# Merged attention heads transposed by TensorE in the query steps, and the first half of feed-forward begun two steps sooner

## The reference

```python
Q, K, V = heads(Wq) / 8, heads(Wk) / 8, heads(Wv)             # heads(W) = x @ W.T, split in 16 heads of 64
def features(z):                                              # 256 features of each token and head
    xw = einsum('bhtd,hmd->bhtm', z, proj)
    xw = xw - max(xw, axis=-1)
    return exp(xw) * exp(-0.5 * sum(z * z)) + 1e-6
phiQ, phiK = features(Q) / 16, features(K) / 16
KV, Ksum = einsum('bhtm,bhtd->bhmd', phiK, V), sum(phiK, axis=2)
num = einsum('bhtm,bhmd->bhtd', phiQ, KV)
den = einsum('bhtm,bhm->bht', phiQ, Ksum) + 1e-6
merged = (num / den) as [tokens, 1024]
x = layernorm(x + merged @ Wo.T + bo)
x = layernorm(x + relu(x @ W1 + b1) @ W2 + b2)
```

## Time and profile before

| | |
|---|---|
| median of 3 runs | 1596.62 us (1596.11 to 1597.07) |
| the profiled execution | 1597.37 us |
| its span, core 2, the slowest | 1595.8 us |
| spans of the eight cores | 1586.9 to 1595.8 us |
| PE busy | 96% of the span |
| ACT, DVE, POOL busy | 46%, 43%, 35% |
| start of step 32, 36, 41, 42, 45 on PE (core 2) | 352, 393.9, 450.1, 461.2, 549.8 us |
| last `up()` ends | 1145.9 us |

### The profile page before, as it was taken

The page is one execution under the profiler, slowest core; times in us unless marked ns, Lnnn a source line. Parts: engine busy times, 40 slices in busy tenths (PEclk is TensorE's granted clock), DMA queues, the critical chain, the costliest instruction groups (busy, mean ns, idle before and its releaser), DMA issues.

```text
span 1595.8 us, 27925 instructions; the slowest of 8 cores (1586.9 to 1595.8 us)
## 1 busy us (share of the span) xinstructions
PE 1535.7 (96%) x9631; PEld 723.0 (45%) x9816; DVE 679.3 (43%) x1385; ACT 729.6 (46%) x1663; POOL 556.5 (35%) x471
## 2 busy tenths in 40 slices
PE   7999999997988899999999999999999999999998
PEld 3455555553434344444444444444444444444443
DVE  4788888887864444444444443100011111111111
ACT  3577777776764555656655565344311111011111
POOL 4466666662435443444434433000021111111110
...
GB/s 183 135 122 108 105 107 130 72 37 135 203 208 208 205 135 195 121 192 139 146 179 132 152 152 186 80 142 152 130 244 161 150 59 165 165 102 123 60 53 40
DMA packets 259433, 219.94 MB, mean 138 GB/s; under 512 B 205280, under 2 KB 205792, under 8 KB 255840
## 3 DMA queue, kind: packets, MB, share of 16 engines
...
## 4 chain that ended last, share of the span: by engine, by line
PE 86%; DMA 4%; DVE 3%; issue 3%; SPq 2%; ACT 2%; POOL 0%; DVEq 0%; ACTq 0%; POOLq 0%
PE bk L73 50%; PE ps L73 35%; SPq L68 2%; DVE maxa L80 2%; DMA eta<-eq 1%; ACT eq L74 1%; DMA wk<-WkT 1%; DMA etb<-eq 1%; ACT e L74 1%; DVE bia L79 0%; DMA x0f<-xT 0%; DVE r L79 0%; DMA r<-x 0%; SPq L62 0%; DMA r1n_d<-r1n 0%
## 5 line engine op out<-in xcount | busy, mean ns | idle before, releaser
L80 DVE TENSOR_REDUCE maxa<-ps 128x4 f32<-128x1024 f32 x256 | 311.5, 1217 | 118.9 <-PE ps L73 118.4
L74 ACT ACTIVATE eq<-ps,bia 128x256 bf16<-128x256 f32 x512 | 200.6, 476 | 218.8 <-DVE bia L79 108.6
L74 ACT ACTIVATE e<-ps,bia 128x256 bf16<-128x256 f32 x512 | 202.4, 487 | 89.0 <-DVE bia L79 85.5
L73 PE MATMUL bk<-rt,w 128*128 128x512 bf16 x1022 | 241.4, 381 | 0.7 <-issue 0.2
L73 PE MATMUL ps<-rt,w 128*128 128x512 bf16 x981 | 234.7, 381 | 3.2 <-issue 1.3
L73 PE MATMUL ps<-w,ht 128*128 128x512 bf16 x1004 | 222.6, 379 | 1.1
L73 PE MATMUL bk<-w,ht 128*128 128x512 bf16 x1003 | 222.4, 379 | 1.1
L74 ACT ACTIVATE jnk<-out,nmu 128x1024 bf16<-128x1024 f32 x32 | 36.7, 1148 | 383.6 <-DVE nmu L78 383.6
L77 POOL TENSOR_TENSOR out<-rn,b2b 128x1024 f32<-128x1024 bf16 x32 | 68.2, 2136 | 361.3 <-DMA out<-out 334.1
L78 POOL TENSOR_SCALAR eq<-eq 128x1024 bf16<-128x1024 bf16 x88 | 92.1, 1046 | 238.3 <-ACT eq L74 238.1
L78 POOL TENSOR_SCALAR e<-e 128x1024 bf16<-128x1024 bf16 x128 | 133.9, 1046 | 104.6 <-ACT e L74 99.6
...
## 6 DMA issues: line engine op xcount, KB each, us to landing
h_d<-hts SPq DMA_DIRECT2D x112, 256.0 KB, 2.6
ht<-h_d SPq DMA_DIRECT2D x14, 2048.0 KB, 15.2
...
r1n_d<-r1n SPq DMA_DIRECT2D x32, 256.0 KB, 2.8
w<-W POOLq DMA_DIRECT2D x4, 2048.0 KB, 16.4
```

The source lines that it names most:

```text
L73: "matmul": lambda g, *a, **k: g.matmul(*a, **k),
L74: "activation": lambda g, *a, **k: g.activation(*a, **k),
L80: "reduce_max": lambda g, *a, **k: g.reduce_max(*a, **k),
```

## The change

Five things, all written into the same lists of instructions:

1. `S_UP` goes from 42 to 40. Steps 40 and on have `up()`: two in step 40, four in step 41, then eight. `up()` 1 to 30 are done by the end of step 44, where 16 were; 42 remain behind step 66, where 56 did. `load_w1`, `load_rt` and the other things tied to `S_UP` move two steps up (`rt0` is loaded at the end of step 39, where it was step 40).
2. `w_step(r)` is r+3 where it was r+4. For the five blocks whose `wo` then falls before step 40 (r = 32 to 36), `transpose_m` is replaced by `transpose_pe`: 8 PE transposes against an identity (`IDN`) into bank 5, and one ACT copy of 128x1024 to `MGT`, at the start of the step of `wo`.
3. In the steps 32 to 39 the projections stand in groups 0 and 1 (they were in 0 and 2) and `wo` in groups 2 and 3 (1 and 3).
4. `eps_row` is spread over the four groups of step 33, in banks 5 and 6 in turn.
5. `warm` has 58 matmuls for 40, and the four W2 loads are issued after 2, 14, 26 and 38 of the 42 last `up()` (8, 20, 32 and 44 of 56).

```diff
@@ -476,14 +479,18 @@
-    S_UP = 42
+    S_UP = 40
 
     def n_step(r):
         return r + 2 if r <= S_UP - 2 else r + 1
 
     def w_step(r):
-        return {S_UP - 3: S_UP, S_UP - 2: S_UP + 1, S_UP - 1: S_UP + 1}.get(
-            r, r + 4 if r < S_UP else r + 2)
+        return {S_UP - 2: S_UP + 1, S_UP - 1: S_UP + 1}.get(r, r + 3 if r < S_UP else r + 2)
+
+    def by_pe(r):
+        return w_step(r) < S_UP
...
+    def transpose_pe(r, b):
+        pe.wait(mrg_ready[r], idn_ready, *free[b])
+        t = BK[b].bitcast(BF16).rearrange("p (c t) -> p c t", c=8)
+        for c in range(8):
+            tok = pe.do("transpose", t[:, c, :], MRG[r % 2][:, c * 128:(c + 1) * 128], IDN[:, :],
+                        mark=(c == 7))
+        act.wait(tok, mgt_done.get(r - 2))
+        tm[r] = act.do("copy", out=MGT[r % 2][:, :, :], in_=t, mark=True)
+        free[b] = (tm[r],)
...
-        return {0: 2 * su, (1 if su == 3 and nt > 10 else 2): 2 * su + 1}
+        return {0: 2 * su, (1 if 32 <= s < S_UP or (su == 3 and nt > 9) else 2): 2 * su + 1}
...
-    for k in range(40):
+    for k in range(58):
         pe.do("matmul", BK[6], WARM[:, 0:128], WARM[:, :], start=True, stop=True)
...
-    ups = {S_UP: 4, S_UP + 1: 4, 64: 12, 65: 12}
+    ups = {S_UP: (0, 0, 1, 1), S_UP + 1: (1,) * 4, 64: (3,) * 4, 65: (3,) * 4}
...
-            if s == 33 and g == 0:
-                eps_row()
             if s < S_UP:
...
-                if g % 2 == 1:
-                    for r in wos:
-                        wo(r, g // 2, 5)
+                if s == 33:
+                    eps_row(g, 5 + g % 2)
                 for r in nums:
                     num(r, g)
+                for r in wos:
+                    if g == 0:
+                        transpose_pe(r, 5)
+                    if g > 1:
+                        wo(r, g - 2, 5)
...
-                if nums:
+                if nums and not by_pe(nums[-1]):
                     transpose_m(nums[-1])
...
-        if up_n[0] - n0 in (8, 20, 32, 44):
+        if up_n[0] - n0 in (2, 14, 26, 38):
             pool.wait(up_tok[0])
-            load_w2((up_n[0] - n0 - 8) // 12)
+            load_w2((up_n[0] - n0 - 2) // 12)
```

More of the change, by code:

```diff
@@ L79 @@
     "scalar_tensor_tensor": lambda g, *a, **k: g.scalar_tensor_tensor(*a, **k),
+    "transpose": lambda g, *a, **k: g.transpose(*a, **k),
     "reduce_max": lambda g, *a, **k: g.reduce_max(*a, **k),
@@ L163, in build_program @@
     IND = small("ind_sb", [128, 2], BF16, 4)
+    IDN = small("idn_sb", [128, 128], BF16, 256)
     ONESR = small("onesr", [1, 128], BF16, 256)
@@ L499, in transpose_e, with eps_row @@
                                EQ[(2 * s + half) % 3][:, :])
-    crow_ready = None
-    def eps_row():
-        nonlocal crow_ready
-        for k in range(4):
-            row = BK[KVBANK][0:1, 0:260]
-            pe.wait(*free[KVBANK], kvr_ready, onec_ready)
-            for c in range(2):
-                tok = pe.do("matmul", row.rearrange("p (h e) -> p h e", e=65), ONEC[:, :],
-                            KVR[:, 4 * k:4 * k + 4, c, 0:65], start=(c == 0), stop=(c == 1),
-                            mark=(c == 1))
-            dve.wait(tok, kvr_ready)
-            t = dve.do("tensor_scalar", out=CROW[:, k, :], in0=row, scalar1=EPS, scalar2=None,
-                       op0=ALU.mult, mark=True)
-            dve.wait(t)
-            crow_ready = dve.do(
-                "tensor_scalar", out=CROW[:, k, :].rearrange("p (h e) -> p h e", e=65)[:, :, 64:65],
-                in0=row.rearrange("p (h e) -> p h e", e=65)[:, :, 64:65], scalar1=EPS,
-                scalar2=256.0 * EPS, op0=ALU.mult, op1=ALU.add, mark=True)
-            free[KVBANK] = (crow_ready,)
+    crow_ready = [None] * 4
+    def eps_row(k, b):
+        row = BK[b][0:1, 0:260]
+        pe.wait(*free[b], kvr_ready, onec_ready)
+        for c in range(2):
+            tok = pe.do("matmul", row.rearrange("p (h e) -> p h e", e=65), ONEC[:, :],
+                        KVR[:, 4 * k:4 * k + 4, c, 0:65], start=(c == 0), stop=(c == 1),
+                        mark=(c == 1))
+        dve.wait(tok, kvr_ready)
+        t = dve.do("tensor_scalar", out=CROW[:, k, :], in0=row, scalar1=EPS, scalar2=None,
+                   op0=ALU.mult, mark=True)
+        dve.wait(t)
+        crow_ready[k] = dve.do(
+            "tensor_scalar", out=CROW[:, k, :].rearrange("p (h e) -> p h e", e=65)[:, :, 64:65],
+            in0=row.rearrange("p (h e) -> p h e", e=65)[:, :, 64:65], scalar1=EPS,
+            scalar2=256.0 * EPS, op0=ALU.mult, op1=ALU.add, mark=True)
+        free[b] = (crow_ready[k],)
     def num(r, k):
@@ L845, in build_program @@
             else:
-                nu = ups.get(s, 8) // 4
+                nu = ups.get(s, (2,) * 4)[g]
                 two = len(nums) == 2
```

13 lines of the change are left out of this document (8 added, 5 removed).

## The result

The changed kernel takes 1614.55 us (median of four runs), the kernel before 1596.74 beside it: a ratio of **1.0107, 95% interval 1.0087 to 1.0127**. The forecast was 1591.2, with a range up to 1600.

A forecast was written before the change was run, and what follows sets the result against it. PE, busy 96%, was taken as the bound, with at most some 32 us to be had. Gains of 5.9 us in steps 33 to 44 and 1 at the start, less 1.5 for W2, gave 5.4: 1591.2 us, range 1581 to 1600.

The forecast's parts named there:

- last W2 load: First `ffn_down` block: load slowed by SP's reads; 2.7 us wait at half speed, bounds none to 8, 1.5 taken.
- -5.9 forecast: Step 33 to the start of step 45: 206.6 us less 24.2 for early `up()`, 182.4 against 188.3.
- 25.8 us idle: Steps 33 to 44 before, on core 2: PE idle 25.8 of 188.3 us.
- 33: Step 33: PE chain of `eps_row` goes, its DVE work stays; 10.7 us for 13.2, bounds 9 and 13.2.
- wait for bank 4: Second projection in steps 34, 35, 37 to 39: PE waits about 2 us for ACT's copy, bounds 1.2 and 2.6.
- 37 to 39: Steps 37 to 39: 13.3 us each, from 11.1 work, 0.4 transposes and 1.8 to 2 wait.
- 40: Step 40, first with `up()`: 16.5 us work, waits some 2 and 5, clock 1.8; 25.3, bounds 18 and 29.
- 41: Step 41: 20.4 us of work and 1.1 of small waits.
- 43: Step 43: `rt1` before a half of `eq`, 2.1 us wait, 25.9 us in all.
- The 5 us stall: Step 43: the 5.15 us PE stall goes, since only step 41 has two `wo` blocks, with residuals fetched earlier.
- Start: Kernel start: 18 more `warm` matmuls, 3.9 us, fill slow cores' gap; slowest core gains 0 to 2, 1 taken.
- rival C: Start of `ffn_down`: W2 lands 14 us or more in, PE stands 10; adds 9 to 12, to 1601; chance 0.14.

The follow-up runs named there:

- e4: The kernel before with only `eps_row` spread over the four groups of step 33, in banks 5 and 6: ratio 0.9997.
- e5: The kernel before with projections in groups 0 and 1 and `wo` in 2 and 3, no PE transposes: 1616.8 and 1619.6 us.
- e18: The kernel before with only `wo` of block 41 moved from step 43 to 44: ratio 1.0002.
- e6: The kernel before with only `warm` at 58 matmuls instead of 40: ratio 1.0003.
- e1: The changed kernel with the W2 loads issued after 0, 10, 20 and 30 of the last 42 `up()`: ratio 1.0058 to the kernel before.
- e3: The kernel before with the W2 loads issued after 16, 28, 40 and 52 of the last 56 `up()`: ratio 1.0051.
- e19: The kernel before with PE transposes in step r+3, `wo` at r+4, and the copy to `MGT` ahead of the group's four exponentials on ACT: ratio 1.0034.

## Why the prediction was wrong

The forecast went the wrong way. It put waits and clock at too little in the steps that were full before, and left one wait out. **The steps of the prediction that failed:** the wait at bank 6 was not in the sum at all (0.75 us in each of steps 34 to 39); the waits for halves of `eq` in steps 41 and 43 were put at small waits and 2.1 us (measured 2.38 and 3.80, with the clock behind); and the last W2 load at 1.5 us (measured 6.0).

It was also worked out for one core. On core 2 steps 33 to 44 took 188.3 us before; in the changed kernel they take 213.1, which less 24.2 is 188.9, +0.6 for the -5.9 forecast. On core 6 they took 184.5, so the 17.7 us between -5.9 and its +11.8 are 13.9 in the steps and 3.8 in the base. The slowest core sets the time, and the change made it another one. And the 25.8 us idle of the prediction are too many: core 2's trace lacks 22 of some 1220 matmul records in this stretch. Core 6 had 21.0 idle, and none of the 1.6 in steps 36 to 41.

Forecast 206.6 us for steps 33 to 44, measured 220.5 on core 6. By step:

- **33 (10.7, measured 11.2).** The chain of `eps_row` went, and the wait for bank 4 came, 1.78 us; the step ends with 2.38 for ACT `eq`, which the sum did not have. Right in size, 0.5 over. That the gain would last was not: by e4 most of it is given back in the next four steps.
- **34 (10.3, 11.9) and 35 (13.3, 14.7).** Mis-sized, and not by the wait forecast: no wait for bank 4 came in either. The clock was granted at 0.79 and 0.82, so that the first projections took 3.38 and 3.60 us for 1.9, and PE waited 0.75 and 1.54 for DVE `mrg` in step 34, 0.75 in step 35. I had counted work and waits and no clock, though the earlier trace rows showed the clock falling around such gaps.
- **36 (11.6, 12.3) and 37 to 39 (39.9, 43.9).** The waits at bank 4 were as forecast (2.22, 1.28, 1.68 for 1.8 to 2), the transposes too (0.54 for 0.4). **A missing term**: 0.75 us at bank 6 in each, and in 34 and 35. With the second projection gone from between them, `num` of group 2 follows that of group 1 after 0.33 us of `features`, while DVE still reads the bank. I had listed what stood between the two projections and not what had stood between the two `num`; e5 has the same 0.75. And 1.53 for the clock in step 37. For the four steps 51.5 was forecast and 56.2 measured; these two terms are 4.5 of the 4.7 between.
- **40 (25.3, 24.8).** Right in size, in part by luck: `rt0` issued 1.7 us into the step (forecast 1.2), landed at +9.6 (9 to 12), the half of `eq` at +17.6 (18.3 to 20). PE waited 3.24 us for `etb` and not 5, none for `rt` where 2 stood in the sum, and in place of these six waits of 0.3 to 0.4 us for DVE `mrg` and ACT `eq` (2.1 in all), which it lacked.
- **41 (21.5, 25.4) and 43 (25.9, 29.2).** **Mis-sized by 3.9 and 3.3.** The 5 us stall went, as forecast. In step 41 I had allowed no wait for DMA at all, though its W1 quarter and half of `eq` stand on SP as in step 40: the half landed 10.5 us after its issue. In step 43 the wait was 3.8 for 2.1, and both had the clock behind them (2.55 us for eight matmuls of 1.89). These two steps vary most from core to core. e18 shows the same exchange, a late half of `eq` in place of a late residual.
- **42 and 44 (24.2 and 23.9, 23.6 and 23.5).** Right.
- **Start (1 us gained, none measured).** By e6 the fill works, and the end stays.
- **Last W2 load (1.5, 6.0; 8 by e1 and e3).** The bounds held the wait (4.48 lies between none and 8), and 2.7 was worked out from half speed. I then took less, "since small reads come first", for which I had no row. The load moved nothing in its first 3 us (before as well: the DMA lines below), so on core 6 by the block's start only 3.7 of its 11.6 us of transfer were done, and the rest took 14.9. The clock behind the wait, 1.5 us, was priced only in rival C. Rival C named the mechanism and the landing (14 us or more after the block's start; it was 14.9), and I gave it 0.14. Its price of 9 to 12 is too high, for a load that lands at 14 is 3.6 us late for a need at 10.4, not 10.

The DMA share by fortieths, before (core 2, 1123 to 1143 us, the load issued at 1125.9) and changed (core 6, 1148 to 1172, issued at 1148.5):

```profile
DMA  0000000000084999899999999999999996000000
```

```profile
DMA  0000037999999999999969899989979999996999
```

The Trainium skill (DMA: Bandwidth & Descriptors, Queues, rings and completion order) says that an engine takes turns between queues by whole packets; on core 6 the load's 14.9 us for what alone took 8 agrees with a share of about a half. But with SP's reads 6.4 us behind its issue on every core, the load landed after 16.4 to 21.1 us, and why the cores differ isn't shown.

What these have in common is where the change put its parts. Steps 36 to 41 had no idle time, so all that is added there counts in full, and the pair of projections and the transposes stood in them: 56.2 us on core 6 for four steps of 11.1, a loss of 11.8 in steps 36 to 39 alone, twice the forecast gain.

Of the transposes, the Trainium skill (TensorE: Matmul & The Clock Gate, Part 4: PE-mode transpose) has about 275 ns each in a kernel, and has them not counted as busy by the clock gate. The row has 0.54 us for eight, 0.068 each; the measurement decides. In e19 the clock was 1.00 over steps 38 to 40 with eight transposes each, so at this number of them no row shows an effect on it.
